# Two message-passing layers over a graph: how many partitions the indirect transfers over the nodes use

## What is computed

```python
# layer 0
h1, h2, h3, h4 = (node_proj(x, W[k], b[k], node_type) for k in (1, 2, 3, 4))
w5e   = edge_attr_16 @ W5[edge_type] + b5[edge_type]
num   = sum(h3[dst] * (h4[src] + w5e), axis=-1)
score = softmax((num / sqrt(16))[:, None], axis=-1)[:, 0]
msg   = score[:, None] * (h2[src] + w5e)
x     = layernorm(x + h1 + segment_sum(msg, dst))
# layer 1
m     = relu(x[src] + (edge_attr_32 @ We + be)) + 1e-7
ez    = exp(m - segment_max(m, dst)[dst])
agg   = segment_sum(m * ez / segment_sum(ez, dst)[dst], dst)
x     = layernorm(x + (x + agg) @ Wm + bm)
```

## Time and profile before

| | |
|---|---|
| time, median of two runs | 1917.71 us |
| span of the profiled execution, first to last instruction | 2193.7 us |
| busy in it: PE, DVE, POOL, ACT | 82%, 75%, 58%, 36% |
| granted TensorE clock, mean | 0.916 of full speed |
| indirect transfers of the four passes | 100 of 1333 |

### The profile page before, as it was taken

One profiled execution on the slowest core, in us unless ns is written; L12 is line 12 of the kernel. 1 busy time (PEld: TensorE's weight loads), 2 busy tenths in 40 slices (PEclk: granted clock), 3 DMA queues, 4 the chain that ended last, 5 costly groups with the idle time before them and its releaser, 6 DMA issues.

```text
span 2193.7 us, 29535 instructions
## 1 busy us (share of the span) xinstructions
PE 1808.2 (82%) x9200; PEld 1086.3 (50%) x9200; DVE 1649.8 (75%) x3316; ACT 791.6 (36%) x1503; POOL 1282.8 (58%) x1347
## 2 busy tenths in 40 slices
PE   6599999999999999999981678788887878879863
PEld 5334555655555655555560245445444544545432
DVE  6534877878878788788787378778887877878876
ACT  3101223223322333223231145455554545545561
POOL 7365666666666666666614666666666666666624
PEclk9899999999999999999995789889998998989975
DMA  8933445554545555555442245555554545555541
GB/s 283 391 61 94 139 144 148 148 151 144 148 142 153 143 146 145 147 148 152 138 141 58 48 134 156 141 151 157 153 149 142 164 140 162 149 149 153 151 140 57
DMA packets 216065, 321.30 MB, mean 146 GB/s; under 512 B 61931, under 2 KB 123940, under 8 KB 215781
## 3 DMA queue, kind: packets, MB, share of 16 engines
q1 hardware_dynamic: 128950, 148.58, 23.3%
q0 software_dynamic: 43056, 68.05, 13.8%
q10 hardware_dynamic: 43904, 102.79, 13.1%
HBM read 186.00 MB, written 133.22 MB: 146 GB/s over the span
## 4 chain that ended last, share of the span: by engine, by line
PE 29%; issue 26%; DVE 16%; another core or an unknown queue 12%; ACT 11%; ACTq 3%; POOL 1%; DMA 1%; SPq 0%; DVEq 0%; POOLq 0%
PE wide L900 11%; PE wide L999 7%; DVE late L1210 3%; ACT block L819 3%; DVE edge_lists L1210 3%; DVE featm L1226 2%; DVE score L1216 2%; ACTq L812 2%; ACT prob_wide L796 2%; PE wide L1010 2%; ACT msg L797 1%; DVE h3d L1235 1%; ACT block L800 1%; PE wide L860 1%
## 5 line engine op out<-in xcount | busy, mean ns | idle before, releaser
L634 POOL DMA_INDIRECT rows<-d_x,idx x588 | 558.3, 950 | 342.1 <-issue 158.2
L624 POOL DMA_INDIRECT block<-d_h,idx x482 | 455.6, 945 | 278.8 <-issue 126.2
L900 PE MATMUL wide<-late,typed 125*128 125x512 bf16 (+1 forms) x936 | 282.4, 382 | 35.7 <-issue 35.3
L999 PE MATMUL wide<-late,ntype_i 125*128 125x512 bf16 x975 | 239.5, 403 | 53.9 <-DVE ntype_i L1346 49.7
L900 PE MATMUL wide<-edge_lists,typed 125*128 125x512 bf16 (+1 forms) x864 | 259.8, 381 | 22.1 <-issue 20.9
L1235 DVE TENSOR_TENSOR_SCAN h3d<-keep,h3d,bank 128x512 f32<-128x512 bf16 x98 | 125.4, 1280 | 176.4 <-issue 171.2
L999 PE MATMUL wide<-edge_lists,ntype_i 125*128 125x512 bf16 x936 | 223.4, 393 | 11.1 <-issue 11.0
L624 POOL DMA_INDIRECT rows<-d_h,idx x160 | 151.0, 944 | 132.7 <-remote 48.4
L1010 PE MATMUL wide<-ident,block 128*128 128x128 f32 x784 | 135.3, 319 | 93.6 <-ACT block L819 59.3
L999 PEld LDWEIGHTS wide<-late,ntype_i 125*128 125x128 bf16 x975 | 100.9, 104 | 175.9 <-DVE ntype_i L1346 50.1
L900 PE MATMUL wide<-late,ntype_i 125*128 125x512 bf16 (+1 forms) x468 | 179.0, 383 | 3.9 <-issue 3.5
(11 more groups left out here) (224 smaller groups left out, 3390.0 us busy)
## 6 DMA issues: line engine op xcount, KB each, us to landing
d_run<-block ACTq DMA_DIRECT2D x98, 512.0 KB
d_inj<-zeros SPq DMA_DIRECT2D x28, 896.0 KB
inj<-d_inj SPq DMA_DIRECT2D x98, 256.0 KB
d_run<-stage ACTq DMA_DIRECT2D x98, 256.0 KB
feat<-in_ea16x3T SPq DMA_DIRECT2D x196, 96.0 KB
types<-d_type SPq DMA_DIRECT2D x196, 64.0 KB
keep<-d_keep SPq DMA_DIRECT2D x196, 64.0 KB
keep<-d_pen SPq DMA_DIRECT2D x196, 64.0 KB
```

Source lines behind the costliest of these rows:

```text
L624: pool.indirect_dma_start(out=ring[c % RING][:, j, h, :], out_offset=None, in_=d_h24, in_offset=bass.IndirectOffsetOnAxis(ap=idx[:, c, at: ...
L634: pool.indirect_dma_start(out=rows1[c % RING1][:, j, h, :], out_offset=None, in_=d_x1, in_offset=bass.IndirectOffsetOnAxis(ap=idx[:, c, at ...
L900: ins = pe.matmul(p_pick[s][:, 0:cols], table0[n][:, k, :], hot0[b][:, k - b * KT, 0:cols], start=(k == 0 and n == 0), stop=(k == NT - 1 a ...
L999: ins = pe.matmul(p_hot[s], table[q][:, SPLIT * k:SPLIT * (k + 1), :].rearrange("p b c -> p (b c)"), hot[s][:, k, :], start=(k == 0 and q ...
```

## The change

The indirect transfers of the four passes no longer use 128 partitions each. Tile i uses 128 - i % 4: tiles 0, 4, ... 24 (seven of them) keep 128, tiles 1, 5, ... 21 (six) use 127, tiles 2, 6, ... 22 (six) use 126, tiles 3, 7, ... 23 (six) use 125. The order of POOL's instructions and everything on the other engines stays. No partition that holds a node is left out.

```diff
+        def rows_of_tile(i):
+
+            return slice(0, P - i % 4)
...
-                pool.indirect_dma_start(out=found_all[:, i, :], out_offset=None, in_=t["dst"],
-                                        in_offset=bass.IndirectOffsetOnAxis(ap=row_i[:, i:i + 1], axis=0)).then_inc(s_got[group_of(i)], 16)
+                pool.indirect_dma_start(out=found_all[rows_of_tile(i), i, :], out_offset=None, in_=t["dst"],
+                                        in_offset=bass.IndirectOffsetOnAxis(ap=row_i[rows_of_tile(i), i:i + 1], axis=0)).then_inc(s_got[group_of(i)], 16)
...
-                pool.indirect_dma_start(out=d_inj, out_offset=bass.IndirectOffsetOnAxis(ap=first_i[:, i:i + 1], axis=0),
-                                        in_=H_all[:, i, 3 * C:4 * C], in_offset=None).then_inc(s_inj, 16)
+                pool.indirect_dma_start(out=d_inj, out_offset=bass.IndirectOffsetOnAxis(ap=first_i[rows_of_tile(i), i:i + 1], axis=0),
+                                        in_=H_all[rows_of_tile(i), i, 3 * C:4 * C], in_offset=None).then_inc(s_inj, 16)
...
-                pool.indirect_dma_start(out=got0_all[:, i, :], out_offset=None, in_=d_run0,
-                                        in_offset=bass.IndirectOffsetOnAxis(ap=last_i[:, i:i + 1], axis=0)).then_inc(s_got[group_of(i)], 16)
+                pool.indirect_dma_start(out=got0_all[rows_of_tile(i), i, :], out_offset=None, in_=d_run0,
+                                        in_offset=bass.IndirectOffsetOnAxis(ap=last_i[rows_of_tile(i), i:i + 1], axis=0)).then_inc(s_got[group_of(i)], 16)
...
-                pool.indirect_dma_start(out=H_all[:, i, 0:2 * C], out_offset=None, in_=d_run1,
-                                        in_offset=bass.IndirectOffsetOnAxis(ap=last1_i[:, i:i + 1], axis=0)).then_inc(s_got[group_of(i)], 16)
+                pool.indirect_dma_start(out=H_all[rows_of_tile(i), i, 0:2 * C], out_offset=None, in_=d_run1,
+                                        in_offset=bass.IndirectOffsetOnAxis(ap=last1_i[rows_of_tile(i), i:i + 1], axis=0)).then_inc(s_got[group_of(i)], 16)
```

## The result

The changed kernel took **1969.35 us** (median of 2 runs, 1968.26 to 1970.43) against 1917.71 us: ratio 1.027, 95% interval 1.024 to 1.030, 51.6 us more. A second measurement of the same kernel gave 1.028 (1.0265 to 1.030), 53.3 us more. The forecast was 1922 us with a range of 1914 to 1950; the time lies above it.

A forecast was written before the change was run, and what follows sets the result against it. PE and DVE carry the long, untouched chunk loops; only passes 3 and 4 were taken as exposed. Pass 3 +1.6 us, pass 4 +3, passes 1 and 2 0: 1917.7 + 4.6 = 1922 us, range 1914 to 1950.

The forecast's parts named there:

- the lower end: POOL's instructions in the four passes: narrowing adds nothing if time goes by rows, 0.6 ns each.
- The upper end: POOL's instructions: time goes by rows of one engine, 9 ns each; 127 partitions +1.1 us, 7.5 us a pass.
- the lumps on the DMA engines: Many rows of one transfer on one DMA engine: 127 rows land 2.8 us later in pass 3, 3.7 in pass 4.
- Fewer engines for one transfer: POOL's DMA queue: 128 rows use 16 engines, 127 one, 126 fourteen, 125 five, by largest divisor up to 16.
- Rival 1: POOL's queue spreads any count over 16 engines, so nothing is narrowed: 1918 us, within 2 us; chance 28%.
- Pass 2: ... against 18 us of cover: 0.: Scatter before PE takes `inj`: under 2 us a lump against about 18 us of cover, so 0.
- what it delays of the other loads I count as up to 1 us: Pass 1: its own lateness is covered (0, 8 us left); delay to other loads up to 1 us.
- Pass 3 +1.6 and pass 4 +3: Gather between the layers and last gather: DVE's waits for late-landing groups move the end by 1.6 and 3 us.
- I add them unscaled: Sum for all passes: +4.6 us of fixed latency, added unscaled to the profile's 2193.7 us and the runs' 1917.7 us.
- Rival 3: POOL handles uneven counts row by row: over 2% (38 us) slower, 2070 us at 50 ns a row; chance 13%.
- rival 2: POOL slows by the rows of one engine, 7.5 us each in passes 3 and 4: +20 us, 1938 us; chance 26%.

The follow-up runs named there:

- ladder: Against the kernel before, only pass 4 narrowed, its 25 tiles using 25 different partition counts from 128 to 16; read for times alone; 1924.16 us in one run.
- only127: Changed kernel with only tiles 1, 5, ... 21 narrowed (127 partitions) in each pass, the rest at 128; 1.0249 of the kernel before, +46.6 us.
- pass2_b: Kernel before with only pass 2 (the scatter) narrowed, where before takes 1918.30 us; ratio 1.0070, +13.6 us.
- hold: Kernel before, 128 partitions everywhere, with POOL fills ahead of tiles 1, 5, ... and 3, 7, ... in all four passes; ratio 1.0131, +25.2 us.
- pass1_b: Kernel before with only pass 1 narrowed, where before takes 1918.30 us; ratio 1.0070, +12.2 us.
- pass4: Kernel before with only pass 4 (the last gather) narrowed, where before takes 1919.31 us; ratio 1.0070, +12.3 us.

## Why the prediction was wrong

- **"I take the lower end for the forecast, as 907 against 944 ns says that the rows are a small part of the instruction."** This step failed first. Its reading was of transfers that use 16 engines, where 8 rows or 4 lie on one; it can't price 127 on one. The upper end had the right form (by the rows of one engine), with 9 ns a row and 7.5 us a pass; measured were 13.5 ns a row and 11.3 us a pass. Between ends far apart, the one whose mechanism was at hand would have been the better choice, as the lumps on the DMA engines were taken from that very mechanism. Passes 3 and 4 cost 24.9 us, where the forecast had 4.6; that alone would have stayed in the range (1943 us), and passes 1 and 2 took the time above it.
- **Fewer engines for one transfer**: right, as far as POOL's times and the packets can tell. 14 engines for 126, 5 for 125 and 1 for 127 fit the ladder's times and those in the changed kernel. Rival 1 (nothing is narrowed) is refuted by `only127`.
- **"Pass 2: ... against 18 us of cover: 0."** Wrong, and the second largest error: `pass2_b` is +13.6 us. The distance from the last scatter to PE's use of `inj` was taken for idle cover. It was a chain: behind SP's wait for pass 2 stand the loads of the pick lists, 10.4 us from issue to landing, then DVE and PE. The step read who uses `inj`, and not what else is queued behind the wait. That the same edit cost 1.9 us on the 2209 us chip is not this cover either: PE stood there too, and the loop of layer 0 took it up.
- **Pass 1**: the cover of POOL's and DVE's time was right (`hold`: 0.8 us late at the first gather). What failed is "what it delays of the other loads I count as up to 1 us": it was 12.2 us, through SP's stores of the lists and of H. That it went over these stores is shown; how a lump slows them is argued.
- **Pass 3 +1.6 and pass 4 +3**: +12.6 and +12.3, nearly all of it POOL's time (12.1 and 12.8 us). The forecast's whole term, the lumps' later landing, was 0.5 us of it in pass 3 instead of 1.6; in pass 4 none is left to see.
- **"I add them unscaled"**, from a profile of 2193.7 us to runs of 1918 us: the gap of 276 us was named and passed over. It was a sign that the profile showed another state of affairs, with PE standing between matmuls (1.97 and 1.73 us at 176 and 179 us, with no named releaser). On the 2209 us chip passes 1 and 2 cost 6.3 and 1.9 us, on the others 12.2 and 13.6.
- **Rival 3** named 2% as reached at x = 2.9 us for a 127 and a 125 together. It was reached at x = 1.85, as pass 2 had no 16 us of cover and pass 1 paid 12.2 us by another way: with no cover the same formula asks 24x = 38, x = 1.6. That number was at hand as the case without cover. So the time fell where rival 3 (13%) had it, by the mechanism of rival 2 (26%), which counted both passes as covered and ended at 1938 us. A slip in rival 3: with its own 50 ns for x = 7.6, x = 2.9 is 19 ns a row, not 23.

## What to carry to other kernels

Before a wait is called covered, list everything that stands behind it in its engine's queue and who waits for each item; the first user of the awaited data isn't always the first to suffer. For an indirect transfer, choose a partition count with a large divisor up to 16: 128, 126 or 112 cost POOL under 1 us here, 127 costs 2.54, and padding rows cost less than dropping them. And where the profiled execution is 14% longer than the runs, find out which loop is longer before any cover in it is counted.

## What was not expected of the hardware

- POOL's time for an indirect transfer grew by 13.5 ns for each row on the engine that has most of them (by the rule for k), on top of 0.94 us at 8 rows; fewer rows gave little (0.86 to 0.91 us for 16, 32, 48, 64 and 80 partitions in `ladder`).
- One chip ran the kernel before in 2209 us where two others took 1918 to 1919, with a granted clock of 0.916 against 0.957 and gaps of 1 to 2 us between single matmuls. What causes those gaps stays open.
- Beside pass 1's transfers of 127 KB, stores of another queue were slower: the issue of two stores of H took 9.3 us in `pass1_b`, 5.0 in `pass4` and 6.5 in `hold`, although POOL's queue moved the same 3.3 MB.
